# A wait for landed rows at every second unit of a gather loop (graph network, layer 3, one Trainium2 core)

## The chip, the cores and the metric

The kernel runs on one core of one Trainium2 chip. The metric is the device time of one execution in microseconds (us), lower is better; for the kernel before it is the median of three runs. A separate execution was recorded by the hardware profiler, and all rows below come from that one.

## The reference, cut to what matters

A four-layer network on a graph of 3125 nodes and 100000 edges, 256 features a node. Every layer has a message pass over the edges, a linear attention over nodes and an expert block. What matters here is layer 3's edge pass, an attention over the edges that end in each node:

```python
logits = leaky_relu(a_s[src] + a_d[dst] + a_e, 0.2)      # 4 heads
m = segment_max(logits, dst);  p = exp(logits - m[dst])
z = segment_sum(p, dst);       alpha = p / (z[dst] + EPS)
out = segment_sum(xp[src] * alpha[:, :, None], dst)       # 256 features
```

So for each edge a row of 256 features (with 8 small columns: ones and scores) is fetched by the number of its source node, scaled by a weight, and added to the row of its destination node.

## The kernel before, in words

The edges are sorted by destination and laid out in columns of 128. Four columns (`G = 4`) are a **unit** of 512 edges whose destinations all lie in one tile of 125 nodes. There are `UNITS_S = 220` units. Layer 3's pass is `build_attend3` (L922 on); it is one block in which each engine runs its own list of instructions, and the engines meet at semaphores.

- **GpSimd** runs `rows_of_unit` (L650 to L659). For unit `u` it waits until unit `u - 11` has been summed (`LANES_B = 11` row buffers, three of them in the spare tile `dst_order_record`, the others named `att_rows`), then issues four indirect DMAs (L658), each of which gathers 128 rows of 1056 bytes from HBM. Each adds 16 to the semaphore `rows_in` of the buffer when it has landed. Nothing else is on GpSimd's list in this pass. The same function fetches rows for layer 0's pass, there with five buffers (`LANES_A = 5`).
- **TensorE** does, at step `i`: `give_back` at every fourth step (L1126, L1128), `add_up(i - 8)` (L1136, which signals `summed`), `find(i + 1)` (L1101, signals `found`), `turn(i + 2)` (L1091, signals `turned`), and `flip` at every fourth step (L1113, L1115).
- **ScalarE** copies each turned mask out of PSUM (`keep_turned`, L1162, waits for `turned`), which `find` of that unit and the next `turn` wait for. It also does the exponentials and scales the sums (L1200, L1203).
- **VectorE** does, at step `i`: `raise_top` and `add` for older units (L1043 to L1056), `weigh(i - 7)` (L1027, L1029), `measure(i)` (L996, waits for the landed rows of unit `i` and for `found`), `make_hot(i + 2)` (L977), and once in four units a maximum over runs of edges (L1011 to L1021).

Thus rows of unit `i` are first read at step `i` and last read at step `i + 8`, and the buffer is filled again for unit `i + 11`: GpSimd may be up to three units ahead of `measure`.

Of the kernel before, what the change touches and what calls it, by code (L numbers as in the profile page):

```python
# [16 lines left out]
G = 4  # L17
# [12 lines left out]
UNITS_S = UNITS_1 + TILES - 1  # L30
# [616 lines left out]
    return eng.value_load(o["tile"][0:1, u:u + 1], min_val=0, max_val=TILES - 1)  # L647


def rows_of_unit(nc, pool, s, table, o, rows, width, lanes):  # L650

    for u in range(UNITS_S):
        l = u % lanes
        if u >= lanes:
            pool.wait_ge(s["summed"], u - lanes + 1)
        for g in range(G):
            k = u * G + g
            nc.gpsimd.indirect_dma_start(rows[l][:, g, 0:width], None, table, bass.IndirectOffsetOnAxis(ap=o["row"][:, k:k + 1], axis=0)  # L658
                                         ).then_inc(s[f"rows_in{l}"], 16)  # L659
# [16 lines left out]
def build_attend0(nc, c, o, table, to_dst, attn, acc, pairs):  # L676
# [9 lines left out]
    with ExitStack() as ctx:  # L686
# [12 lines left out]
        with phase(nc, "att0", *names) as s, nc.Block() as block:  # L699
# [6 lines left out]
            @block.gpsimd  # L706
            def _(pool):
                rows_of_unit(nc, pool, s, table, o, rows, W, LANES_A)
# [163 lines left out]

BATCH = 4
LANES_B = 11
WAITS = 7
SUMS_WAIT = WAITS + 1
HOTS_B = SUMS_WAIT + 3
# [35 lines left out]
def batch_of(u):  # L913
    return u // BATCH
# [7 lines left out]
def build_attend3(nc, c, o, table, to_dst, attr, slope, top, acc, last):  # L922
# [9 lines left out]
    W = E + H  # L932
# [4 lines left out]
    with ExitStack() as ctx:  # L937
# [5 lines left out]
        rows = [spare[:, l * lane:(l + 1) * lane].rearrange("p (g w) -> p g w", g=G) for l in range(in_spare)]  # L943
        rows += [sb(f"rows{l}", [P, G, W + 1])[:] for l in range(in_spare, LANES_B)]
        hot = [sb(f"hot{l}", [P, G, R]) for l in range(HOTS_B)]
# [14 lines left out]
        with phase(nc, "att3", *names) as s, nc.Block() as block:  # L960
            @block.gpsimd
            def _(pool):
                rows_of_unit(nc, pool, s, table, o, rows, W, LANES_B)

            @block.vector
            def _(dve):
# [22 lines left out]
                def measure(u):  # L989

                    b, j = batch_of(u), u % BATCH
                    dve.wait_ge(s[f"rows_in{u % LANES_B}"], 16 * G * (u // LANES_B + 1))
                    dve.wait_ge(s["found"], u + 1)
                    if b >= 2:
                        dve.wait_ge(s["flipped"], b - 1)
                    v.tensor_tensor(score[b % 2][:, :, j * H:j * H + H], rows[u % LANES_B][:, :, E:W], found[u % 2][:, :, 0:H], ALU.add).then_inc(s["measured"], 1)  # L996

# [17 lines left out]
                def bound_back(b):  # L1015

                    n = H * (last_of(b) % BATCH + 1)
                    dve.wait_ge(s["ran"], b + 1)
                    v.tensor_tensor_scan(high[0:n, ::-1], apart[0:n, K:0:-1], run[0:n, ::-1], 0.0, ALU.add, ALU.max).then_inc(s["ran_back"], 1)
                    dve.wait_ge(s["ran_back"], b + 1)  # L1020
                    v.tensor_tensor(run[0:n, :], score_p[0:n, :], high[0:n, :], ALU.subtract).then_inc(s["bounded"], 1)  # L1021

                def weigh(u):

                    l, b, j = u % LANES_B, batch_of(u), u % BATCH
                    dve.wait_ge(s["back_ready"], b + 1)
                    v.tensor_tensor(rows[l][:, :, E:W + 1], back[b % 2][:, :, BATCH + j, :], col_of(last[:, u * G:u * G + G], H + 1), ALU.mult)  # L1027
                    part = rows[l][:, :, 0:E].rearrange("p g (h x) -> p g h x", h=H)
                    v.tensor_tensor(part, part, back[b % 2][:, :, j, 0:H].unsqueeze(3).to_broadcast([P, G, H, C + 1]), ALU.mult).then_inc(s["scaled"], 1)  # L1029
# [32 lines left out]
                for i in range(N + SUMS_WAIT + 4):  # L1062
                    if 0 <= i - SUMS_WAIT - 2 < N:
                        raise_top(i - SUMS_WAIT - 2)
                    if i % BATCH == 1 and 0 < i // BATCH <= B:
                        bound_back(i // BATCH - 1)
                    if 0 <= i - WAITS < N:
                        weigh(i - WAITS)
                    if i < N:
# [2282 lines left out]
```

## Time and profile before

| | us |
|---|---|
| median of 3 runs | 9703.57 (9694.26 to 9703.69) |
| span of the profiled execution | 10401.4 |
| layer 3's edge pass in that span, first gather to last matmul of the pass | 8043.9 to about 9580 |

The profiled execution is 697.8 us (7.2%) longer than the median of the plain runs; the page has no plain time for it, and no row says in which stages the difference lies. Over the whole span TensorE is busy 61%, VectorE 47%, GpSimd 43% and ScalarE 20%. A row of a timeline has the start in us from the span's start, the duration in us, the engine and line, the operation with the tiles it writes and reads, and in brackets how long the engine was idle before it and whose semaphore ended that. "issue" there means that nothing in the profile is shown as the cause. PEclk is the granted TensorE clock as a share of full speed (2.4 GHz).

### The profile page before, as it was taken

What the parts mean: (1) busy time and instruction counts of PE and PEld (TensorE: products, weight loads), DVE (VectorE), ACT (ScalarE), POOL (GpSimd) and SP (SyncE); (2) the same over time, 40 slices, a digit from 0 to 9 for tenths busy, and PEclk for the clock granted to TensorE, in tenths of its full rate; (3) what the DMA queues carried; (4) which work ended last, traced back from release to release, by engine and by line L of the source; (5) the groups of instructions that cost most, each with busy time, mean ns of one, the idle gap of its engine ahead of it and who ended that gap; (6) DMA issues with size and microseconds to landing.
All of it is one profiled execution on the core that took longest, in us unless ns stands there. A gap on an engine that the chain in (4) does not pass through costs nothing. (4 is left out here: it accounts for less than half of the span.)

```text
span 10401.4 us, 95746 instructions
## 1 busy us (share of the span) xinstructions
PE 6311.5 (61%) x28050; PEld 4795.7 (46%) x28050; DVE 4856.6 (47%) x13537; ACT 2031.2 (20%) x5038; POOL 4458.2 (43%) x4412
## 2 busy tenths in 40 slices
PE   0001115999996865454665444453965788887699
PEld 0000004888884433333443333342863676776466
DVE  7561216888884532222242222264113566666633
ACT  0000002444443210000120000012212232232322
POOL 0546772666660036666104666602020566664000
PEclk9998557999997986666676666675987777777799
DMA  0001002333330133333102333301960232222000
GB/s 12 6 1 28 7 4 71 83 83 83 83 83 14 46 108 92 94 92 92 35 11 70 94 92 92 92 18 25 316 221 27 77 81 80 80 81 64 11 13 19
DMA packets 404431, 697.45 MB, mean 67 GB/s; under 512 B 154143, under 2 KB 267784, under 8 KB 403421
## 3 DMA queue, kind: packets, MB, share of 16 engines
q0 software_dynamic: 206848, 480.68, 17.1%
q1 hardware_dynamic: 197076, 210.68, 6.3%
q8 instruction: 236, 3.87, 0.2%
q14 instruction: 271, 2.22, 0.1%
HBM read 631.46 MB, written 59.47 MB: 66 GB/s over the span
## 5 line engine op out<-in xcount | busy, mean ns | idle before, releaser
L658 POOL DMA_INDIRECT att_rows<-el_table,dst_order_row x1520 | 1589.4, 1046 | 1067.4 <-issue 387.0
L641 PE MATMUL sum_sum<-sum_rows,sum_hot 128*125 128x256 f32 x3520 | 1227.5, 487 | 1291.4 <-issue 817.1
L641 PEld LDWEIGHTS sum_sum<-sum_rows,sum_hot 128*125 128x125 f32 x3520 | 824.8, 240 | 1694.4 <-issue 1540.9
L602 POOL DMA_INDIRECT sum_rows<-rel_table,src_order_row x880 | 833.0, 947 | 1042.3 <-ACTq L593 629.2
L602 POOL DMA_INDIRECT sum_rows<-el_table,dst_order_row x880 | 833.0, 947 | 956.7 <-ACTq L593 543.7
L554 POOL DMA_INDIRECT dst_order_record<-records,dst_order_row x784 | 813.7, 1038 | 589.2 <-PEq L458 297.1
L624 DVE TENSOR_TENSOR gnn_acc<-gnn_acc,sum_sum 125x256 f32 x440 | 180.6, 410 | 1888.8 <-DMA ffn1e_w<-in_L_ffn_W_dram 938.7
L1136 PE MATMUL att_sum<-att_rows,att_hot 128*125 128x265 f32 x1280 | 429.3, 492 | 36.4 <-ACT att_part L1203 30.5
L800 PE MATMUL att_found<-gnn_to_dst,att_hot_t 125*128 x1760 | 437.8, 392 | 2.5 <-ACT att_hot_t L849 1.8
L658 POOL DMA_INDIRECT dst_order_record<-el_table,dst_order_row x240 | 266.1, 1109 | 400.4 <-SPq L960 240.5
L824 PE MATMUL att_sum<-att_rows,att_hot 128*125 128x261 f32 x1760 | 427.3, 385 | 2.4 <-ACT att_rows L862 2.4
L862 ACT ACTIVATE att_rows<-att_rows,att_p 128x257 f32<-128x257 f32 x880 | 375.8, 498 | 0.0
L1101 PEld LDWEIGHTS att_found<-layer_a_dst,att_hot_t 125*128 125x128 f32 x1760 | 275.9, 227 | 180.6 <-issue 159.4
L1136 PEld LDWEIGHTS att_sum<-att_rows,att_hot 128*125 128x125 f32 x1280 | 293.4, 241 | 114.7 <-issue 46.9
L1101 PE MATMUL att_found<-layer_a_dst,att_hot_t 125*128 x1760 | 254.4, 268 | 140.1 <-issue 84.2
L800 PEld LDWEIGHTS att_found<-gnn_to_dst,att_hot_t 125*128 125x128 f32 x1760 | 319.7, 192 | 38.0 <-issue 3.1
L824 PEld LDWEIGHTS att_sum<-att_rows,att_hot 128*125 128x125 f32 x1760 | 314.2, 188 | 47.8 <-ACT att_rows L862 2.5
L744 DVE CUSTOM_DVE_ANT_0 att_high<-att_high,att_att 128x256 f32<-128x256 f32 x880 | 320.0, 418 | 0.0
L1162 ACT COPY att_hot_t<-att_turn_p 125x512 f32<-125x512 f32 x220 | 129.1, 587 | 802.7 <-PE att_turn_p L1091 461.7
L809 PE MATMUL att_spread_p<-ident,att_score 128*125 128x128 f32 x1760 | 251.6, 286 | 43.2 <-issue 27.2
L739 DVE TENSOR_TENSOR att_high<-att_rows,att_found 128x1024 f32<-128x1024 f32 x220 | 268.7, 1222 | 6.5 <-issue 6.5
L809 PEld LDWEIGHTS att_spread_p<-ident,att_score 128*125 128x125 f32 x1760 | 210.0, 188 | 130.6 <-issue 85.1
(775 smaller groups left out, 12593.2 us busy)
## 6 DMA issues: line engine op xcount, KB each, us to landing
block_w<-in_L_ffn_W_dram SPq DMA_DIRECT2D x112, 512.0 KB, 6.3
block_w<-in_L_ffn_W_dram SPq DMA_DIRECT2D x56, 1024.0 KB
att_rows<-el_table,dst_order_row POOLq DMA_INDIRECT x1520
rel_table<-open_st SPq DMA_DIRECT2D x25, 784.0 KB
sum_rows<-rel_table,src_order_row POOLq DMA_INDIRECT x880
sum_rows<-el_table,dst_order_row POOLq DMA_INDIRECT x880
dst_order_record<-records,dst_order_row POOLq DMA_INDIRECT x784
pairs<-zeros SPq DMA_DIRECT2D x1, 7168.0 KB
```

The costliest lines, as they stand in the source:

```text
L554: nc.gpsimd.indirect_dma_start(o["record"][:, k, :], None, o["records"], bass.IndirectOffsetOnAxis(ap=o["row"][:, k:k + 1], axis=0)).then_ ...
L602: nc.gpsimd.indirect_dma_start(rows[l][:, g, :], None, table, bass.IndirectOffsetOnAxis(ap=o["row"][:, k:k + 1], axis=0)).then_inc(s[f"row ...
L641: last = nc.tensor.matmul(slot(u), hot[u % HOTS_S][:, g, :], rows[l][:, g, :], start=(g == 0), stop=(g == G - 1))
L658: nc.gpsimd.indirect_dma_start(rows[l][:, g, 0:width], None, table, bass.IndirectOffsetOnAxis(ap=o["row"][:, k:k + 1], axis=0)).then_inc(s ...
L739: v.tensor_tensor(high[:], rows[u % LANES_A][:, :, 0:D], found[:], ALU.max).then_inc(s["picked"], 1)
L744: last = v.tensor_tensor_reduce(high[:, g, :], high[:, g, :], att[:], 0.8, 0.0, ALU.mult, ALU.add, score[u % 2][:, g:g + 1])
L800: last = t.matmul(found[:, g, :], hot_t[u % TURNED][:, g * P:(g + 1) * P], nodes_of_unit(to_dst, tile), start=True, stop=True)
L809: last = t.matmul(spread_p[:, g * P:(g + 1) * P], score[u % 2][:, g:g + 1].to_broadcast([P, R]), c["ident"][:], start=True, stop=True)
L824: last = t.matmul(sums[u % 2][:, 0:S], hot[u % HOTS][:, g, :], rows[u % LANES_A][:, g, :], start=(g == 0), stop=(g == G - 1))
L862: last = a.activation(own_rows[:, g, 0:D + 1], own_rows[:, g, 0:D + 1], ACT.Copy, scale=p[u % 2][:, g:g + 1])
L1101: done = t.matmul(found[u % 2][:, g, 0:H], hot_t[u % 2][:, g * P:(g + 1) * P], nodes_of_unit(to_dst, tile), start=True, stop=True)
L1136: done = t.matmul(sums[u % SUMS_B][:, 0:W + 1], hot[u % HOTS_B][:, g, :], rows[u % LANES_B][:, g, :], start=(g == 0), stop=(g == G - 1))
```

## The change

`rows_of_unit` gets a parameter `rest`. Before the gathers of each unit `u` that is a multiple of `rest` (not unit 0), GpSimd waits until all four gathers of unit `u - 1` have landed. Layer 3 passes `REST_B = 2`; layer 0 leaves it at 220, so that it never applies there.

```diff
-def rows_of_unit(nc, pool, s, table, o, rows, width, lanes):
+def rows_of_unit(nc, pool, s, table, o, rows, width, lanes, rest=UNITS_S):
 
     for u in range(UNITS_S):
         l = u % lanes
         if u >= lanes:
             pool.wait_ge(s["summed"], u - lanes + 1)
+        if u and u % rest == 0:
+            before = u - 1
+            pool.wait_ge(s[f"rows_in{before % lanes}"], 16 * G * (before // lanes + 1))
         for g in range(G):
...
+REST_B = 2
...
-                rows_of_unit(nc, pool, s, table, o, rows, W, LANES_B)
+                rows_of_unit(nc, pool, s, table, o, rows, W, LANES_B, REST_B)
```

## Rows read from the trace of the kernel before

**Rows 1.** Windows, two passes: each engine's busy us (count), PEclk, DMA share, GB/s

```profile
1750.00:3150.00 1400.00, 1342.30 (x7754) 1123.69 (x7754) 1145.76 (x4313) 672.84 (x1942) 846.24 (x851) 1.00 0.30 82
8130.00:9545.00 1415.00, 1176.78 (x5860) 1007.86 (x5859) 957.92 (x3087) 426.23 (x1465) 937.11 (x835) 0.77 0.30 81
```

**Rows 2.** Timeline: start, duration, engine, line; GpSimd opening layer 3's pass

```profile
8043.88 0.97 POOL L658 DMA_INDIRECT dst_order_record<-el_table,dst_order_row  x1 [240.50 <-SPq L960]
...
8048.13 0.95 POOL L658 DMA_INDIRECT dst_order_record<-el_table,dst_order_row  x1 [0.30 <-issue]
...
8098.10 0.95 POOL L658 DMA_INDIRECT att_rows<-el_table,dst_order_row  x1 [0.30 <-issue]
8128.57 0.94 POOL L658 DMA_INDIRECT dst_order_record<-el_table,dst_order_row  x1 [29.53 <-PE att_sum L1136]
```

**Rows 3.** Timeline, VectorE, measuring the same first units

```profile
8050.92 0.17 DVE L996 TENSOR_TENSOR att_score<-dst_order_record,att_found 128x16 f32<-128x16 f32 x1 [5.04 <-DMA dst_order_record<-el_table,dst_order_row]
...
8103.90 0.17 DVE L996 TENSOR_TENSOR att_score<-att_rows,att_found 128x16 f32<-128x16 f32 x1 [28.83 <-DMA combine_rows<-results,ffn_place]
...
8134.89 0.16 DVE L996 TENSOR_TENSOR att_score<-att_rows,att_found 128x16 f32<-128x16 f32 x1
```

**Rows 4.** Timeline, TensorE and ScalarE, same stretch

```profile
8063.50 1.20 PE L1091 MATMUL att_turn_p<-ident,att_hot 128*125 128x128 f32 x4
8085.62 1.86 PE L1101 MATMUL att_found<-layer_a_dst,att_hot_t 125*128 x8 [20.93 <-issue]
8087.34 1.20 PE L1091 MATMUL att_turn_p<-ident,att_hot 128*125 128x128 f32 x4
...
8084.90 0.58 ACT L1162 COPY att_hot_t<-att_turn_p 125x512 f32<-125x512 f32 x1 [23.12 <-DMA combine_rows<-results,ffn_place]
8105.95 0.58 ACT L1162 COPY att_hot_t<-att_turn_p 125x512 f32<-125x512 f32 x1 [20.47 <-DMA combine_rows<-results,ffn_place]
```

**Rows 5.** Timeline, mid pass: TensorE, ScalarE, VectorE and GpSimd

```profile
8691.13 0.95 PE L1101 MATMUL att_found<-layer_a_dst,att_hot_t 125*128 x8
8691.94 0.68 PE L1091 MATMUL att_turn_p<-ident,att_hot 128*125 128x128 f32 x4
...
8701.56 1.22 PE L1101 MATMUL att_found<-layer_a_dst,att_hot_t 125*128 x5 [6.31 <-ACT att_hot_t L1162]
...
8700.83 0.58 ACT L1162 COPY att_hot_t<-att_turn_p 125x512 f32<-125x512 f32 x1 [7.76 <-DMA combine_rows<-results,ffn_place]
...
8700.83 0.17 DVE L996 TENSOR_TENSOR att_score<-att_rows,att_found 128x16 f32<-128x16 f32 x1 [2.02 <-issue]
...
8689.26 0.94 POOL L658 DMA_INDIRECT att_rows<-el_table,dst_order_row  x1 [1.09 <-DMA results<-block_y]
...
8698.04 1.60 POOL L658 DMA_INDIRECT att_rows<-el_table,dst_order_row  x1 [0.30 <-issue]
8701.16 1.25 POOL L658 DMA_INDIRECT att_rows<-el_table,dst_order_row  x1 [1.52 <-DMA results<-block_y]
```

**Rows 6.** Groups of instructions, 8100 to 9500: busy us, mean ns, idle before

```profile
L658 POOL DMA_INDIRECT att_rows<-el_table,dst_order_row x583 | 654.7, 1123 | 335.8 <-issue 166.7 <-PE att_sum L1136 127.7 <-DMA results<-block_y 41.4
...
L658 POOL DMA_INDIRECT dst_order_record<-el_table,dst_order_row x228 | 254.2, 1115 | 156.5 <-PE att_sum L1136 71.0 <-issue 64.3 <-DMA results<-block_y 21.3
```

**Rows 7.** VectorE's waits, 8100 to 9500: us in total, times, longest

```profile
DVE att_score L996 <- issue: 220.8, 103, 4.8
DVE att_apart L1011 <- ACT att_high L1179: 90.4, 29, 8.4
```

**Rows 8.** Layer 0's edge pass: one wait row, then one GpSimd timeline row

```profile
ACT att_hot_t L849 <- PE att_turn_p L790: 333.3, 214, 1.9
...
2414.90 0.94 POOL L658 DMA_INDIRECT att_rows<-el_table,dst_order_row  x1 [1.56 <-PE att_sum L824]
```

**Rows 9.** Timeline, the pass's last gather

```profile
9542.48 1.42 POOL L658 DMA_INDIRECT att_rows<-el_table,dst_order_row  x1 [0.30 <-issue]
```

## Prediction

> **What bounds the kernel now.** I read layer 3's pass first by windows, then the engines' timelines at its start, then the waits of its long middle, and last layer 0's pass as a counterpart that uses the same gather function. The windows row of the pass [rows 1] shows no engine full: of 1415 us TensorE is busy 1177, VectorE 958, GpSimd 937, and TensorE's granted clock is 0.77 of full speed. Layer 0's pass in the row above has TensorE busy 1342 of 1400 us at a clock of 1.00. So layer 3's pass is made of waits between engines, and the question is which ones.
>
> **The start shows it at its plainest.** GpSimd issues the 44 gathers of the eleven free buffers without a pause, one each 1.25 us, from 8043.88 to 8098.10 [rows 2]. The rows land quickly: unit 0's last gather starts at 8048.13 and `measure`, which has waited for it, runs at 8050.92, that is 2.8 us from issue to use, or 1.85 us after the gather's own 0.95 us [rows 2, 3]. But TensorE's signals to the others are late. A turn that starts at 8063.50 and takes 1.20 us is followed by ScalarE's copy only at 8084.90, 20.2 us later; a find that ends at 8087.48 by VectorE's measure only at 8103.90, 16.4 us later; the turn at 8087.34 by the copy at 8105.95 [rows 3, 4]. Nothing else stands ahead of those instructions on their engines, which are idle for 15 to 29 us. The lateness ends a few us after GpSimd's last gather. Unit 4 is therefore measured at 8103.90 and unit 10 at 8134.89, although its rows landed at about 8101 [rows 2, 3].
>
> **The middle shows the same in small.** In a stretch of eight gathers (8689.26 to 8699.64) a find and a turn end at 8692.1 and 8692.6; ScalarE's copy and VectorE's measure both start at 8700.83, in GpSimd's pause of 1.52 us, and TensorE goes on at 8701.56 after 6.31 us idle [rows 5]. Over 8100 to 9500 VectorE waits 220.8 us in 103 places before `measure` and 90.4 us before L1011, none of it put down to landed rows [rows 7]. In layer 0's pass GpSimd pauses 1.56 us after every four gathers, and the longest wait of ScalarE's copy for TensorE's turn is 1.9 us in 214 [rows 8]. The traces thus speak for a rule of this kernel: TensorE's signals reach the others late while gathers follow each other without a pause, and on time where GpSimd pauses after each unit. Why is not shown.
>
> **The change part by part.** It adds 109 waits on GpSimd (even units 2 to 218) and removes nothing. Behind each are four gathers, on whose landing `measure` of that unit waits; GpSimd has no other work. The wait itself costs the landing: 1.85 us from the end of the last gather, about 1.95 with the semaphore's way, in place of an issue gap of 0.30. That is 1.65 us more for each pair of units, where `summed` had not made GpSimd pause anyway.
>
> *Start, units 0 to 10.* Five waits (units 2, 4, 6, 8, 10) move the last gather from 8098.10 to 8098.10 + 5 x 1.65 = 8106.4, and unit 10's rows land at 8109.2. It was measured at 8134.89, so up to 25.7 us are free. GpSimd's next step, unit 11, was released by `summed` of unit 0 at 8128.57 [rows 2], 29.5 us after the last gather; now it could come at 8106.4 + 1.25 = 8107.6 if unit 0 is summed by then, a gain of 20.9 us. It needs TensorE's signals to come through in each pause, with ten us between two pauses and eight steps to do in 55 us. I take -20 us. Bounds: -26, and +8.3 (5 x 1.65) if the signals owed nothing to the gathers.
>
> *Middle, units 11 to 219.* From 8128.57 to 9542.48 are 208.75 units [rows 2, 9], so 6.77 us a unit, 13.55 a pair. GpSimd's own need now: gathers of 1.12 us (583 of 1123 ns, 228 of 1115) [rows 6] and gaps of 0.30, 5.7 us a unit. With the wait a pair needs 8 x 1.12 + 7 x 0.30 + 1.95 = 13.0 us, 6.51 a unit. That still fits under 6.77. GpSimd idles in the middle for `summed` already: 127.7 + 71.0 + 41.4 + 21.3 us, the 71.0 with the start's 29.5 in it [rows 2, 6], so that some pauses are merely moved. The two bounds: if TensorE's signals cost nothing any more, the pass falls to GpSimd's floor, (6.77 - 6.51) x 208.75 = -54 us; if every added pause lies on the path, 104 x 1.65 = +172 us. The rows lie nearer the first: the rows come ahead of use by up to three units (20 us), the idle time of 220.8 + 90.4 us on VectorE is there to be won, and the counterpart with a pause at every unit has no late signals. But the wait stands only at even units, so eight gathers in a row remain allowed, the very length that holds signals back for 8 us [rows 5]. Only longer stretches are excluded, and some of the eights are cut in two. I take half of the floor's gain, -27 us.
>
> *Sum.* -20 - 27 = -47 us of the profiled 10401.4, so 10354. The plain runs are 0.933 of the profiled time, and I scale the gain by it: -44, 9703.6 - 44 = 9660 us. After the pass nothing depends on its inner order, so the gain is kept.
>
> The Trainium skill ("DMA: Bandwidth & Descriptors", section "Rules for kernel authors") says to issue a DMA early and wait for its semaphore late, so that its fixed cost is hidden. This change does the reverse on the issuing engine; by that rule alone the result is rival B. The trace agrees with the rule as far as rows are concerned (no wait for them in the middle), but not that issuing ahead is free. The same page ("Anatomy of one DMA — SWDGE (gpsimd) path") fits 2.0 us plus bytes/436e3; for 135 KB that gives an estimate of 2.3 us from issue to landing where the rows here show 2.8, and the pair would need 12.5 us.
>
> **Rivals.**
> - *A. Signals are freed altogether.* GpSimd's floor decides: -20 - 54 = -74, scaled -69: 9634 us. For it: layer 0's pass [rows 8]. Against: eights remain. 17%.
> - *B. GpSimd becomes the bound; slower.* If the pause and longer gathers bring a pair over 13.55 us (a pause over 2.5 us, or gathers of 1.19 us on average), or if the pauses for `summed` stay where they are, at the other units, the added ones come on top. With half of them on the path: 86 - 20 = +66, scaled +61: 9765 us. For it: only 4% of room a pair (13.0 of 13.55), and gathers of 1.60 us do occur [rows 5]. Against: three units of lead. 15%.
> - *C. The late signals are the profiler's.* The recorded execution is 7% longer than the plain ones; if TensorE's signals are late only under recording, plain runs gain nothing, and the start loses 5 x 1.65 us: 9711 us, within 0.2% or a little over. 17%.
> - *D. Only the start gains.* In the middle the pauses replace each other: -20, scaled -19: 9685 us. 18%.
> - That the change doesn't act is excluded by the rows: 1.95 us after an odd unit's last gather is more than the 0.30 us seen at most of them.
>
> **How the numbers follow.** Forecast (start and half the floor) 33%, A 17%, D 18%, C 17%, B 15%. About 0.2% (19 us) is what a measurement of this kernel can tell from no change. Faster: forecast, A, and half of D, 0.59. Same: half of D, most of C, 0.21. Slower: B and the rest of C, 0.20. The range reaches over A and C, and to a small B of a quarter of the pauses (43 - 20 = +23, scaled +21, 9725): 9612 to 9735.
>
> **What would show it.** Right: GpSimd's timeline has a gap of about 1.95 us before the gathers of units 2, 4, 6, 8, 10; ScalarE's copies of the first units follow TensorE's turns by a few us; unit 11 is fetched near 8108; VectorE's wait before `measure` falls well below 220 us, and TensorE's granted clock is over 0.77; no stretch has over eight gathers. Wrong: the copies still come 10 to 20 us late across pauses (then the start keeps its time), a wait of `measure` for landed rows (B), or a shorter profiled span with an unchanged plain median (C).

## The result, and the profile after

The changed kernel takes 9935.5 us (median of 4 runs, 9928.3 to 9943.5) against 9698.9 us for the kernel before: ratio 1.0249, interval 1.0235 to 1.0264, or +237 us. The forecast was 9660 us, faster; the result lies outside its range, on the other side. Its profiled execution spans 9934.9 us, the same as its plain runs, whereas that of before had spanned 10401.4 us for plain runs of 9699 us. So before was recorded once more, and all comparisons below use this **second recording of before**, which spans 9698.2 us.

Groups of instructions in the middle of the pass (line, engine, operation, count | busy us, mean ns of one | idle us before them and what ended it), first the kernel after, 7600 to 9080 us:

```profile
L661 POOL DMA_INDIRECT att_rows<-el_table,dst_order_row x610 | 713.1, 1169 | 367.0 <-issue 167.8 <-DMA att_rows<-el_table,dst_order_row 167.8 <-DMA dst_order_record<-el_table,dst_order_row 26.3
L661 POOL DMA_INDIRECT dst_order_record<-el_table,dst_order_row x228 | 266.1, 1167 | 135.1 <-issue 60.9 <-DMA dst_order_record<-el_table,dst_order_row 42.5 <-DMA att_rows<-el_table,dst_order_row 21.2
```

and the second recording of before, 7600 to 8840 us:

```profile
L658 POOL DMA_INDIRECT att_rows<-el_table,dst_order_row x608 | 674.9, 1110 | 229.2 <-issue 165.5 <-PE att_sum L1136 63.7
L658 POOL DMA_INDIRECT dst_order_record<-el_table,dst_order_row x227 | 252.5, 1113 | 85.0 <-issue 62.2 <-PE att_sum L1136 22.8
```

Nearly the same gathers (838 and 835) take 1480 us in the one and 1240 us in the other. GpSimd accounts for it by itself: its idle time grew from 314.2 to 502.1 us (+187.9) and the gathers' own time from 927.4 to 979.2 us (+51.8), +239.7 in all. These rows answer to [rows 6], where the first recording had 156.5 + 335.8 us idle. GpSimd used to be stopped by `summed` (86.5 us); now landed rows stop it (257.8 us).

VectorE's waits (us in total, times, longest), 7650 to 8750 us, after and then the second recording of before:

```profile
DVE att_score L1000 <- DMA att_rows<-el_table,dst_order_row: 252.5, 84, 5.2
DVE att_score L1000 <- DMA dst_order_record<-el_table,dst_order_row: 95.3, 32, 4.2
```

```profile
DVE att_score L996 <- issue: 114.0, 81, 3.4
DVE att_apart L1011 <- ACT att_high L1179: 95.0, 46, 2.2
DVE att_score L996 <- DMA att_rows<-el_table,dst_order_row: 2.5, 2, 2.0
```

After, `measure` waits 347.8 us in all for landed rows, and it has no other waits in the list; before, 2.5 us for them. This is the sign that the prediction gave for rival B. The row answering to [rows 1] says that no engine is full after either. Windows, 7650 to 8750 us (busy us and count of TensorE, its weight loads, VectorE, ScalarE and GpSimd; granted clock as a share of 2.4 GHz; DMA share; GB/s), second recording of before, then after:

```profile
7650.00:8750.00 1100.00, 997.72 (x5154) 869.01 (x5154) 840.38 (x2718) 382.71 (x1288) 819.92 (x741) 0.79 0.34 92
```

```profile
7650.00:8750.00 1100.00, 882.08 (x4353) 760.42 (x4352) 709.78 (x2298) 320.21 (x1092) 724.91 (x623) 0.77 0.29 77
```

**The start**, which was to win 20 us. In the second recording of before, one turn of TensorE and the copy of ScalarE that waits for it (timeline: start, duration, engine, line):

```profile
7556.44 1.22 PE L1091 MATMUL att_turn_p<-ident,att_hot 128*125 128x128 f32 x4 [1.10 <-DVE att_hot L977]
```

```profile
7557.69 0.59 ACT L1162 COPY att_hot_t<-att_turn_p 125x512 f32<-125x512 f32 x1 [4.21 <-PE att_turn_p L1091]
```

The turn ends at 7557.66 and the copy starts 0.03 us later, while GpSimd gathers without a pause. In the first recording the turn of the same unit was followed by its copy 20.2 us late [rows 4]. The first gather starts at 7538.63, and unit 10 is measured at 7600.57, 62 us on; in the first recording that was 91 us [rows 2, 3]. Unit 11's first gather, which in the first recording came after 29.5 us of idle time, follows the one before it with the usual gap:

```profile
7598.97 0.95 POOL L658 DMA_INDIRECT dst_order_record<-el_table,dst_order_row  x1 [0.30 <-issue]
```

There was nothing to win.

### The profile page after: what moved, and what is told of

It reads as the page before. It is cut to its first block and busy times, and to the rows that moved or that the text cites. A ratio compares the mean times of both kernels' runs of the same rounds, so it can differ in the third digit from the quotient of the medians.

```text
span 9934.9 us, 95850 instructions
## 1 busy us (share of the span) xinstructions
PE 6331.6 (64%) x28050; PEld 4844.5 (49%) x28050; DVE 4857.6 (49%) x13537; ACT 2036.2 (20%) x5038; POOL 4530.2 (46%) x4412
## 5 line engine op out<-in xcount | busy, mean ns | idle before, releaser
L661 POOL DMA_INDIRECT att_rows<-el_table,dst_order_row x1520 | 1622.1, 1067 | 956.2 <-issue 379.6
L641 PE MATMUL sum_sum<-sum_rows,sum_hot 128*125 128x256 f32 x3520 | 1267.1, 523 | 957.7 <-DMA sum_rows<-el_table,dst_order_row 471.3
L641 PEld LDWEIGHTS sum_sum<-sum_rows,sum_hot 128*125 128x125 f32 x3520 | 868.6, 259 | 1356.3 <-issue 1009.4
L602 POOL DMA_INDIRECT sum_rows<-rel_table,src_order_row x880 | 835.3, 949 | 895.6 <-ACTq L593 627.9
L602 POOL DMA_INDIRECT sum_rows<-el_table,dst_order_row x880 | 835.9, 950 | 807.6 <-ACTq L593 539.8
L554 POOL DMA_INDIRECT dst_order_record<-records,dst_order_row x784 | 835.8, 1066 | 582.9 <-PEq L458 297.0
L793 PE MATMUL att_turn_p<-ident,att_hot 128*125 128x128 f32 x880 | 155.1, 299 | 380.8 <-DVE att_hot L671 369.8
L1095 PE MATMUL att_turn_p<-ident,att_hot 128*125 128x128 f32 x880 | 195.0, 356 | 309.9 <-DVE att_hot L981 309.9
L793 PEld LDWEIGHTS att_turn_p<-ident,att_hot 128*125 128x125 f32 x880 | 113.5, 188 | 422.5 <-DVE att_hot L671 422.4
L1095 PEld LDWEIGHTS att_turn_p<-ident,att_hot 128*125 128x125 f32 x880 | 146.9, 237 | 323.1 <-DVE att_hot L981 323.1
```

The costliest lines, as they stand in the source:

```text
L554: nc.gpsimd.indirect_dma_start(o["record"][:, k, :], None, o["records"], bass.IndirectOffsetOnAxis(ap=o["row"][:, k:k + 1], axis=0)).then_ ...
L602: nc.gpsimd.indirect_dma_start(rows[l][:, g, :], None, table, bass.IndirectOffsetOnAxis(ap=o["row"][:, k:k + 1], axis=0)).then_inc(s[f"row ...
L641: last = nc.tensor.matmul(slot(u), hot[u % HOTS_S][:, g, :], rows[l][:, g, :], start=(g == 0), stop=(g == G - 1))
L1095: done = t.transpose(turn_p[:, g * P:(g + 1) * P], hot[u % HOTS_B][:, g, :], c["ident"][:])
```

## The experiments

All differences are to the kernel before as timed alongside each kernel (medians of 9692.3 to 9698.9 us). "Pass" is from the start of layer 3's first gather to that of its last in the recording; "pause" is GpSimd's usual idle time at a new wait. Pass and time don't grow by quite the same amount: one is a single recording, the other a median, and the first gather starts anywhere from 7520 to 7539 us in the eleven later recordings, though no work before it was changed. Differences of a few us between the growth of the pass and that of the time are therefore not to be read.

| kernel | waits | time us | difference (95%) | pass us | pause us |
|---|---|---|---|---|---|
| before, second recording | 0 | 9700.3 | | 1300.6 | |
| the change | 109 | 9935.5 | +2.49% (2.35 to 2.64) | 1547.5 | 2.58 |
| every fourth unit | 54 | 9820.5 | +1.28% (1.11 to 1.45) | 1424.4 | 2.56 |
| every unit | 219 | 10142.7 | +4.58% (4.40 to 4.75) | 1758.8 | 2.56 |
| rows of two units before | 109 | 9698.6 | +0.02% (-0.07 to 0.12) | 1300.6 | |
| three gathers a unit, no wait | 0 | 9690.8 | -0.08% (-0.18 to 0.02) | 1295.8 | |
| three gathers a unit, the change | 109 | 9706.3 | +0.10% (0.00 to 0.19) | 1306.0 | 2.55 |
| wait behind the first gather | 109 | 9704.5 | +0.10% (0.00 to 0.19) | 1317.3 | 0.8 |
| units 2 to 10 only | 5 | 9708.6 | +0.13% (0.03 to 0.22) | 1307.4 | 2.08 |
| the two waits in the other order | 109 | 9822.4 | +1.30% (1.13 to 1.47) | 1436.0 | 2.09 |
| behind the first gather, every unit | 219 | 9810.8 | +1.25% (1.08 to 1.41) | 1423.7 | 0.8 |

**1. The kernel before, recorded again** (no edit).

> The kernel before, unchanged, recorded once more, because its first recording spans 10401.4 us where its plain runs take 9699, while the changed kernel's recording spans 9934.9 us where its runs take 9936. Theory P (the late TensorE signals belonged to that one recording, GpSimd is near its limit without them): the span is near 9700 us, ScalarE's copies follow TensorE's turns within 0.1 us of the signal, VectorE's measure waits for landed rows or hardly at all, and layer 3's gathers span about 1547.5 - 237 = 1311 us (5.96 us a unit). Theory S (signals are really late while gathers follow without a pause): the span is again near 10400, or it is near 9700 and the copies of the first units still come 10 to 20 us late.

Span 9698.2 us, pass 1300.6 us. From unit 11's first gather (7598.97) to the last gather (8839.20) are 208.75 units, so 5.94 us a unit, not the 6.77 of the first recording. The copies follow the turns at once. Theory P holds: the late signals and the 10401 us belong to the first recording alone. Each of the eleven later recordings (this one, the change, and the nine kernels below) spans the time of the plain runs of its kernel to within 0.12%, and in none of them is ScalarE idle for more than 7.3 us before a copy of units 1 to 11, against 23.12 and 20.47 us in the first recording [rows 4]. What disturbed the first recording stays open.

**2. Every fourth unit, every unit.**

```diff
-REST_B = 2
+REST_B = 4
```

In the second kernel it is 1.

> The wait stands at every fourth unit (54 waits for 109). In the changed kernel the 109 waits cost 237 us, 2.2 us each, about the pause of 2.6 us less the gap of 0.3 us. Theory P (GpSimd is the bound from the first wait on): the cost goes with the count, 54 x 2.2 = +117 us, 9817 us. Theory Q (the kernel before has slack on GpSimd that the first waits use up): less than half of that, 0 to +50 us. Theory S: faster than before.

> The wait stands at every unit (219 waits). Theory P: 219 x 2.2 = +476 us, 10175 us. Theory Q (a slack of x us is used up once): more than double the cost of 109 waits, over +500 us. If part of the cost were once for all, at the start or by a change of rhythm, it would be less than +400 us.

+123 us for 54 waits (2.28 each), +237 for 109 (2.17), +445 for 219 (2.03). The cost goes roughly with the count, as P said to within 6 us for the first and 31 for the second, and none of the counts helps. But a fixed price per wait is not the cause, as experiments 4 and 5 show, and that it fits here is in part chance. In the kernel with 54 waits GpSimd's list for four units is 16 gathers, 15 gaps of 0.30 us and a pause of 2.56 us. With the gathers of before (1.11 us) that is 24.8 us, 6.20 a unit, and would cost about +55 us; the gathers came to 1.18 us instead, which makes 6.49, and 6.52 was measured. So about half of the +123 us is longer gathers.

**3. The same waits, for the rows of two units before.**

```diff
-            before = u - 1
+            before = u - 2
```

> The same number of waits at the same units, but each waits for the rows of the unit two before, whose gathers were issued at least four gathers (5.0 us and more) earlier, longer than the 2.8 us from issue to landing. Theory P (the cost is GpSimd standing still until its own last gather has landed): the wait is over when it is reached, +0 to +10 us. Theory R (the instruction itself, or ordering by landed data, costs): up to the 237 us of the change.

+1 us, pass 1300.6 us, the same as before. The instruction costs nothing, and neither does having rows landed in order: the cost comes only where GpSimd stands still until its own last gather has landed.

**4. Three gathers a unit, without and with the change.** In units 11 to 219 of this pass the fourth column keeps stale rows, so a quarter of the rows is left out. With the change, the new wait counts three gathers in the same way.

```diff
-        for g in range(G):
+        for g in range(G if lanes < 11 or u < lanes else G - 1):
...
-                    dve.wait_ge(s[f"rows_in{u % LANES_B}"], 16 * G * (u // LANES_B + 1))
+                    dve.wait_ge(s[f"rows_in{u % LANES_B}"], 16 * (G + (G - 1) * (u // LANES_B)))
```

> The kernel before with three gathers a unit in place of four once each buffer has been filled (units 11 to 219 of layer 3's pass; the fourth column keeps stale rows, so a quarter of the fetched rows is left out). It takes work from GpSimd alone: 1.41 us a unit of its 5.64. In the second recording of before the pass takes 5.94 us a unit, of which TensorE is busy 5.38. Theory P (GpSimd's list is the bound of before, or shares it with TensorE): faster, 40 to 110 us, TensorE then decides. If another engine alone is the bound of before: no change. Theory Q (before has slack on GpSimd) also says no change.

> The changed kernel (wait at every second unit) with the same three gathers a unit. GpSimd's need for a pair is then 6 x 1.15 + 5 x 0.30 + 2.6 = 11.0 us, 5.5 a unit, less than the 5.94 of before. Theory P (the waits cost only because GpSimd's list is full): the difference to the three-gather kernel without waits is far below the 237 us of the change, 0 to +80 us, and the result is not slower than before. If the landing stood on the path by itself, whatever GpSimd's load: again about +237 us over the three-gather kernel.

The first expectation was wrong: with a quarter less on GpSimd the pass is 5 us shorter and the kernel 8 us, not clear of no change, where P expected 40 to 110. GpSimd is not the bound of before; with its list a quarter shorter the loop of the other engines still takes 5.92 us a unit. What sets the 5.92 no run shows; TensorE is busy for 5.39 of the 5.94 us of before (997.72 of 1100 us in the window above). GpSimd's own list, four gathers of 1.11 us and four gaps of 0.30, is 5.64: close behind. The second was right: with room on its list GpSimd pauses 109 times for 2.55 us, and it costs 15 us, 10 of them at the start; from unit 11 on both kernels go at 5.92 us a unit. So waits of the same count and length cost 237 us, or next to nothing beyond the start's 10, by what else is on GpSimd's list. VectorE's waits for rows (7650 to 8750 us) with three gathers and the change:

```profile
DVE att_score L1000 <- issue: 114.3, 83, 3.4
DVE att_apart L1015 <- ACT att_high L1183: 91.2, 45, 2.2
DVE att_score L1000 <- DMA att_rows<-el_table,dst_order_row: 3.9, 2, 2.7
```

These are before's rows again, to a few us.

**5. The wait behind the first gather, at every second and at every unit.**

```diff
-        if u and u % rest == 0:
-            before = u - 1
-            pool.wait_ge(s[f"rows_in{before % lanes}"], 16 * G * (before // lanes + 1))
         for g in range(G):
+            if g == 1 and u and u % rest == 0:
+                before = u - 1
+                pool.wait_ge(s[f"rows_in{before % lanes}"], 16 * G * (before // lanes + 1))
```

> The changed kernel with the wait moved behind the first of the even unit's four gathers: same count, same landing waited for, but one gather (0.30 + about 1.0 us) of the pause is filled. Theory P: the idle gap shrinks from 2.6 to about 1.3 us and the cost from 237 to 109 x (1.3 - 0.3) = 109 us, 9807 us. If the count of waits and not their length decided, 237 us stays.

> The wait behind the first gather, at every unit. Theory of two limits (the engines' loop at 5.92 us a unit, as with three gathers, and GpSimd's own list): the list needs 4 x 1.13 + 3 x 0.30 + 0.80 = 6.22 us a unit, over the loop by 0.28 against the 5.94 of before, so +58 us, 9757 us, although the same wait at every second unit cost 6 us. If each such wait simply cost what it cost at every second unit, twice that: +12 us.

The first gave +6 us where P, with a price per wait, expected +109. The timeline (GpSimd, then VectorE's `measure` of the awaited unit) shows a pause of 0.79 us, not 1.3:

```profile
8000.08 0.95 POOL L661 DMA_INDIRECT dst_order_record<-el_table,dst_order_row  x1 [0.30 <-issue]
...
8001.34 0.95 POOL L661 DMA_INDIRECT att_rows<-el_table,dst_order_row  x1 [0.30 <-issue]
...
8002.84 0.17 DVE L1000 TENSOR_TENSOR att_score<-dst_order_record,att_found 128x16 f32<-128x16 f32 x1 [1.48 <-DMA dst_order_record<-el_table,dst_order_row]
...
8003.07 0.94 POOL L661 DMA_INDIRECT att_rows<-el_table,dst_order_row  x1 [0.79 <-DMA dst_order_record<-el_table,dst_order_row]
```

The list then needs 8 x 1.13 + 7 x 0.30 + 0.80 = 11.9 us for a pair, 5.97 a unit, only just over the loop's 5.92; 6.01 was measured. At every unit the same wait crosses the limit at full price: +118 us, 6.50 us a unit. The expectation of +58 had the sign and the bend right and the size half: it took gathers of 1.13 us and pauses of 0.80, and their means came to 1.19 and 0.85, which makes 6.49. Two limits, of which the longer decides, explain both; a price per wait explains neither.

**6. Only the five waits of the start.**

```diff
-        if u and u % rest == 0:
+        if u and u < lanes and u % rest == 0:
```

> The waits at units 2, 4, 6, 8 and 10 alone, the five that were forecast to win 20 us. Theory P: 5 x 2.2 = +11 us, with unit 10 measured about 72 us after the pass's first gather in place of 62. Theory S (the waits let TensorE's signals through): -20 us.

+10 us, pass +6.8 us, and unit 10 is measured 72.2 us after the first gather, as P expected. The part that was forecast at -20 us costs 10, near the other bound of the prediction (+8.3).

**7. The two waits of an even unit in the other order.** In the changed kernel units 2 to 10 pause for 2.07 to 2.14 us, the units from 12 on for 2.5 and more; from unit 11 on the wait for `summed` stands beside the one for rows.

```diff
-        if u >= lanes:
-            pool.wait_ge(s["summed"], u - lanes + 1)
         if u and u % rest == 0:
             before = u - 1
             pool.wait_ge(s[f"rows_in{before % lanes}"], 16 * G * (before // lanes + 1))
+        if u >= lanes:
+            pool.wait_ge(s["summed"], u - lanes + 1)
```

> The changed kernel with its two waits of an even unit written in the other order, rows first, summed second. In the changed kernel GpSimd starts 0.74 us after the last landing where both waits stand (units 12 on), its wait for rows being an instruction of its own, and after a pause of 2.07 us in all at units 2 to 10, where the wait rides on the gather; the kernel with the wait behind the first gather starts 0.26 us after the landing. Theory T (the 0.48 us belongs to the wait being an instruction of its own, the one written second): pauses of 2.1 us in place of 2.6, 104 x 0.48 = 50 us less than the change, about 9886 us. If the order does not matter: 9936 us.

A little over half the cost is left: +130 us in place of +237. GpSimd and `measure` released by the same landing, in the change and then in the other order:

```profile
8202.39 0.96 POOL L661 DMA_INDIRECT att_rows<-el_table,dst_order_row  x1 [0.30 <-issue]
...
8205.23 0.17 DVE L1000 TENSOR_TENSOR att_score<-att_rows,att_found 128x16 f32<-128x16 f32 x1 [1.17 <-DMA att_rows<-el_table,dst_order_row]
...
8205.94 1.38 POOL L661 DMA_INDIRECT att_rows<-el_table,dst_order_row  x1 [2.60 <-DMA att_rows<-el_table,dst_order_row]
```

```profile
8211.17 0.95 POOL L661 DMA_INDIRECT att_rows<-el_table,dst_order_row  x1 [0.30 <-issue]
...
8213.97 0.17 DVE L1000 TENSOR_TENSOR att_score<-att_rows,att_found 128x16 f32<-128x16 f32 x1 [1.13 <-DMA att_rows<-el_table,dst_order_row]
...
8214.21 0.95 POOL L661 DMA_INDIRECT att_rows<-el_table,dst_order_row  x1 [2.08 <-DMA att_rows<-el_table,dst_order_row]
```

GpSimd is 0.71 us behind VectorE in the one and 0.24 in the other. The trace of the change has an instruction of its own for the wait written second (engine, operation, count: duration in ns, first and last start):

```profile
L658 POOLq EVENT_SEMAPHORE  x104: 17/17/17, 7611.4 to 9068.9; - x104
```

There it waits for landed rows, and the gather behind it for `summed`; in the other order it waits for `summed`, and the gather itself for landed rows. The pause shrinks by 0.49 us, 104 times: 51 us, as expected. The other 56 us or so are the gathers, which went back from a mean of 1166 ns to 1100 (880 x 0.066 = 58 us). That was not expected.

The gathers' rows answering to the first fence, in the other order, 7600 to 8960 us:

```profile
L661 POOL DMA_INDIRECT att_rows<-el_table,dst_order_row x604 | 664.6, 1100 | 326.4 <-issue 157.5 <-DMA att_rows<-el_table,dst_order_row 136.2 <-DMA dst_order_record<-el_table,dst_order_row 18.8
L661 POOL DMA_INDIRECT dst_order_record<-el_table,dst_order_row x228 | 250.1, 1097 | 120.3 <-issue 60.3 <-DMA dst_order_record<-el_table,dst_order_row 39.7 <-DMA att_rows<-el_table,dst_order_row 19.7
```

They are 69 ns shorter than in the change, with the same gathers and the same two waits; what differs is the order of the waits, and with it the moment at which GpSimd starts again.

## Why the prediction was wrong

- **The step that failed is the 6.77 us a unit** of [rows 2, 9], against which GpSimd's need was held. It came from a recording 698 us longer than the plain runs, and the prediction scaled its gain by 0.933 as if the surplus were spread evenly. It was not: 198 us of it lay in this pass (1498.6 against 1300.6 us). The plain kernel goes at 5.94. The prediction's own need of 6.51 us with the waits would then have read as +0.57 x 208.75 = +119 us, slower.
- **"It still fits under"** was the right test with the wrong number. Experiment 4 shows that the test decides: with room the waits cost 15 us, without it 237.
- **The pause of 1.95 us** was 2.58: 0.14 more for the restart at units 2 to 10, and another 0.48 from unit 12 on, where the wait is the second before the same gather. Worth 0.63 x 104 = 66 us.
- **Gathers of 1.12 us** became 1.166 us, and with 1.108 in the second recording that is 0.058 x 880 = 51 us (0.046 x 836 = 38 us against the number used). The sum with these terms: 119 + 66 + 38 + 10 for the start = 233 us. The pass grew by 246.9 us in the recordings and the kernel by 237; the 14 us of the pass that are left have no term here.
- **The rule of late signals** was read rightly from its rows but was the recording's. Rival C said so and got 17%; its price of +8 us for the start was right (+10), but it left out that then GpSimd's list is the longer one in the middle. C and B were one case, not two. Where the surplus sat could not be read from the first recording alone. Beside the second one it is plain: layer 0's pass, with its regular 1.56 us pause [rows 8], was hardly slowed (1426.1 against 1418.8 us), but it began 203 us later, and the two passes that gather at L602 without a pause took 1245 us each in place of 1104. With the 198 us of layer 3 that is 691 of the 703 us between the two recordings.
- **Rival B** named the place (GpSimd the bound, `measure` waiting for landed rows) and the point (a pair's need over the pair's time), with a price of +61 at 15%, a quarter of what came. The point was set at 13.55 us a pair; it is at 11.9.
- **Rivals A and D** rest on the same late signals and fall with them. TensorE's granted clock was to rise over 0.77; it is 0.77 after, and 0.79 in the second recording of before. Of the signs named for it, three came, and none of them speaks for a gain: the gap ahead of the even units, the end of stretches longer than eight gathers, and copies that follow the turns, which they do without the waits too. Unit 11 is fetched 71 us after the first gather, where the forecast had 64 and the second recording of before has 60. `measure`'s waits rose, and they are for landed rows, the sign against it.
- The rule of the Trainium skill ("DMA: Bandwidth & Descriptors", section "Rules for kernel authors"), issue early and wait late, was cited as the one that speaks against the change. The runs agree: 109 waits for the unit two before cost nothing (+1 us), and 109 for the gather just issued cost 237 us, 2.2 each, where GpSimd's list is full.

## What to carry to other kernels

Hold a recording's span against the plain median before building a sum on it; where they differ by 7%, the surplus sits somewhere, and a need that is compared with a stage's time needs that time from the plain kernel. For a wait added to a gathering engine, compare its list (gathers, gaps, pause) with the time a unit takes: in these runs 109 waits cost 15 us below that and 237 above it. If a queue must pause for its own transfers, let it wait for an older one, or issue one more gather first (+6 us here at every second unit, +118 at every unit); and where two waits stand before one instruction, write first the one that ends last.

## What the runs showed of the hardware that was not expected

- A wait for landed rows costs GpSimd 0.74 us from the last landing to the next gather when it is written second of two, and 0.26 us when it is the only one or the first (medians, by the semaphores' times in the recordings; the rows of experiment 7 show it as 0.71 and 0.24 behind VectorE).
- The length of a gather on GpSimd (0.94 us at least) goes with what VectorE does beside it. After the change about two in five of the gathers that follow a pause fall in with VectorE's wide work and take over 2.4 us:

```profile
8218.91 0.68 DVE L1025 TENSOR_TENSOR att_run<-att_score_p,att_high 16x512 f32<-16x512 f32 x1
8219.47 2.86 POOL L661 DMA_INDIRECT att_rows<-el_table,dst_order_row  x1 [2.56 <-DMA att_rows<-el_table,dst_order_row]
...
8219.60 1.22 DVE L1033 TENSOR_TENSOR dst_order_record<-dst_order_record,att_back 128x1040 f32<-128x1040 f32 x1
```

Gathers of over 2 us are not new, and they are not where most of the added time sits: there are 53 in the second recording of before (up to 2.39 us) and 53 after the change (up to 2.99), while those of 1.3 to 2 us rose from 69 to 166. From unit 11 on, VectorE's L1033, L981 and L1060 (L1029, L977 and L1056 before) run beside the gathers of over 2 us for 97% of their time after and all of it before, and beside those of up to 1.1 us for 36 and 37% of theirs.

The Trainium skill ("SBUF — State Buffer", section "SBUF: two separate sides") says that GpSimd cannot write DMA descriptors while VectorE holds the port pair that they share, which it says of VectorE's 2-port modes. Its section "Who interferes with whom" says that `tensor_tensor`, which L1033 and L981 are, has no such mode, so the rule does not account for these gathers. No run here took that VectorE work away; that it lengthens the gathers, and how, is argued and not shown.
